# Attention on one core: a long row's scores in two joined PSUM banks, short rows and queries in a third, two banks for turned probabilities, and the inverse of long sums on GpSimd

## What is computed

```python
q = (xn @ Wq).reshape(b, n, 16, 64).transpose(0, 2, 1, 3) * 64 ** -0.5
k, v = xn @ Wkv split in two, with a null key and a null value in front
sim = einsum('bhid,bjd->bhij', q, k) + bias        # bias: 16 x 1024 x 1024
sim = where(causal, neg, sim); sim = where(mask, sim, neg)
out = einsum('bhij,bjd->bhid', softmax(sim), v)
out = layernorm(out.reshape(b, n, 1024) @ Wo)
```

## Time and profile before

| what | value |
|---|---|
| runs | 1057.35, 1048.52, 1049.11 us (median 1049.11) |
| profiled execution: span | 1055.2 us; of the runs 1057.35 us lies next above it, 2.1 us around the span |
| busy in the span | PE 88%, DVE 76%, ACT 70%, POOL 57% |
| attention with scores ahead, 64.4 to 603.5 us of the span | 539.1 us |

### The profile page before, as it was taken

One profiled execution on the slowest core, in us unless ns is written; L12 is line 12 of the kernel. 1 busy time (PEld: TensorE's weight loads), 2 busy tenths in 40 slices (PEclk: granted clock), 3 DMA queues, 4 the chain that ended last, 5 costly groups with the idle time before them and its releaser, 6 DMA issues. The chain is left out here.

```text
span 1055.2 us, 22432 instructions
## 1 busy us (share of the span) xinstructions
PE 932.6 (88%) x6180; PEld 811.6 (77%) x6180; DVE 803.2 (76%) x2324; ACT 735.9 (70%) x1651; POOL 606.0 (57%) x699
## 2 busy tenths in 40 slices
PE   7899999999999999999999966887976762599997
PEld 5578888888888898998888755677964652499996
DVE  7579989899898898998888879774757786344443
ACT  2268888888888998998999937434764652466663
POOL 2368777777776666775555525481066277344444
PEclk8879999999999999999999986888988885699999
DMA  9156656666666566675665440155864523254453
GB/s 309 44 175 180 189 171 189 178 181 180 176 184 182 170 197 182 187 199 167 182 189 171 137 150 1 51 167 148 282 178 157 205 102 138 88 78 78 73 84 48
DMA packets 111427, 162.14 MB, mean 154 GB/s; under 512 B 16201, under 2 KB 85193, under 8 KB 110282
## 3 DMA queue, kind: packets, MB, share of 16 engines
q1 hardware_dynamic: 100200, 140.56, 45.1%
q0 software_dynamic: 10224, 18.00, 8.2%
q10 hardware_dynamic: 882, 2.14, 0.6%
HBM read 110.31 MB, written 25.17 MB: 128 GB/s over the span
## 5 line engine op out<-in xcount | busy, mean ns | idle before, releaser
L2375 POOL TENSOR_SCALAR probs<-probs,inv_sum 128x1024 f32<-128x1024 f32 (+3 forms) x128 | 301.7, 2370 | 174.2 <-DVE inv_sum L2526 174.2
L2421 ACT ACTIVATE probs<-probs,neg_max 128x1025 f32<-128x1025 f32 (+7 forms) x256 | 197.5, 772 | 30.9 <-DVE neg_max L2486 29.8
L2508 DVE TENSOR_TENSOR pT_lo<-t_ps,pT_hi 128x512 fp32r<-128x512 f32 (+1 forms) x320 | 202.5, 633 | 21.3 <-ACT pT_hi L2403 20.8
L2590 PE MATMUL t_ps<-ident,probs 128*128 128x128 f32 x1152 | 179.9, 274 | 1.1 <-DVE pT_lo L2508 1.1
L2610 PE MATMUL o_ps<-pT_hi,values 128*128 128x256 f32 x576 | 175.0, 323 | 5.2 <-DVE pT_lo L2508 3.5
L2403 ACT ACTIVATE pT_hi<-t_ps 128x512 fp32r<-128x512 f32 (+1 forms) x320 | 175.5, 549 | 5.5 <-PE t_ps L2590 2.3
L2486 DVE CUSTOM_DVE_ANT_0 probs<-s_ps,bias_set,neg_null 128x512 f32<-128x512 f32 (+3 forms) x256 | 164.2, 642 | 4.5 <-PE s_ps L2559 2.6
L2590 PEld LDWEIGHTS t_ps<-ident,probs 128*128 128x128 f32 x1152 | 141.9, 141 | 31.4 <-DVE pT_lo L2508 2.7
L2611 PE MATMUL o_ps<-pT_lo,values 128*128 128x256 f32 x576 | 150.4, 281 | 0.0
L2558 PE MATMUL s_ps<-k_hi,q_hilo 128*128 128x512 f32 (+3 forms) x384 | 143.8, 375 | 4.2 <-PEq L2730 1.4
L2559 PE MATMUL s_ps<-k_lo,q_one 128*128 128x512 f32 (+3 forms) x384 | 135.4, 353 | 0.0
(11 more groups left out here) (385 smaller groups left out, 2124.7 us busy)
## 6 DMA issues: line engine op xcount, KB each, us to landing
bias_set<-bias_dram SPq DMA_DIRECT2D x16, 1024.0 KB, 5.5
bias_set<-bias_dram SPq DMA_DIRECT2D x16, 896.0 KB, 5.4
bias_set<-bias_dram SPq DMA_DIRECT2D x16, 768.0 KB, 4.9
bias_set<-bias_dram SPq DMA_DIRECT2D x16, 640.0 KB, 4.7
q_hilo<-q_hi SPq DMA_DIRECT2D x128, 64.0 KB, 2.0
q_hilo<-q_lo SPq DMA_DIRECT2D x128, 64.0 KB, 2.0
q_one<-q_hi SPq DMA_DIRECT2D x128, 64.0 KB, 2.0
bias_set<-bias_dram SPq DMA_DIRECT2D x16, 512.0 KB, 5.5
```

The lines of the kernel that those rows point to most:

```text
L2375: last = pool.tensor_scalar(keys, keys, inv_sum[:, x.set, unit, h:h + 1], None, ALU.mult)
L2421: act.activation(p, p, ACT.Exp, scale=-1.0, bias=neg_max[:, x.set, row.unit, h:h + 1], accum_out=row_sum[:, x.set, row.unit, h:h + 1]).the ...
L2508: dve.tensor_tensor(pT_lo[n % 3][:, 0:count, :], t_ps[TURNS["slot", n] % 3][:, 0:2 * P * count].rearrange("p (n q) -> p n q", n=count), pT ...
L2590: last = pe.transpose(t_ps[at % 3][:, P * (2 * m + h):P * (2 * m + h) + P], probs_row(x, row, h)[:, 1 + P * (k + m):1 + P * (k + m) + P], ...
```

## The change

- The PSUM banks are dealt out anew. `s_ps` (2 banks in a ring) and `t_ps` (3) become `long_ps` (one tile over two banks), `short_ps` (one bank) and `t_ps` (2).
- A long row of one head is scored in one piece: PE writes both chunks to `long_ps`, and one instruction of DVE (now L2502) reads up to 1024 columns, with no `part_max`. It is at slot 1 for head 0 and slot 3 for head 1.
- Short rows are at slots 2 and 4 in `short_ps`. The query uses `short_ps` too, is made for step g+3 in place of g+4, after the turn of slot 0; ACT and DVE read it in slot 1. Once a round `short_ps` takes the transposed null weights.
- `long_ps` and `short_ps` are single: a writer waits until the last use was read. With two `t_ps`, `turn(n+2)` now waits for `low(n)`.
- DVE inverts short rows only. For a long row POOL itself raises each head's sum to the power -1 and then multiplies.
- Exponentials and results on ACT come one slot later where the scores do.

```diff
-QLEAD = 4
+QLEAD = 3
...
-    for _i, _t in enumerate((0, 0, 1, 2, 3, 4)):
-        SCORES_AT[max(-1, SLOTS_A_STEP * (_x - LEAD) + _t)].append(("s", _x, _i))
+    for _t, (_unit, _h) in enumerate(((LONG, 0), (SHORT, 0), (LONG, 1), (SHORT, 1)), 1):
+        _n = max(-1, SLOTS_A_STEP * (_x - LEAD) + _t)
+        FILLS_AT[_n].append((_unit, _x, _h))
     if _x >= FIRST_Q:
-        SCORES_AT[max(-1, SLOTS_A_STEP * (_x - QLEAD) + 2)].append(("q", _x))
+        QUERY_AT[max(-1, SLOTS_A_STEP * (_x - QLEAD))].append(_x)
...
-        s_ps = [psum(st, f"s_ps{i}", [P, CW]) for i in range(2)]
-        t_ps = [psum(st, f"t_ps{i}", [P, CW]) for i in range(3)]
+        long_ps, short_ps = psum(st, "long_ps", [P, 2 * CW]), psum(st, "short_ps", [P, CW])
+        t_ps = [psum(st, f"t_ps{i}", [P, CW]) for i in range(2)]
...
# POOL, normalise(g, unit)
-                    for h in range(2) if unit == 0 else ():
-                        keys = probs_row(x, row, h)[:, 1:]
-                        last = pool.tensor_scalar(keys, keys, inv_sum[:, x.set, unit, h:h + 1], None, ALU.mult)
-                        last.then_inc(normed, 1)
+                    for h in range(2) if unit == LONG else ():
+                        pool.wait_ge(probs_ready, 4 * g + 2 * h + 1)
+                        inv = inv_sum[:, x.set, unit, h:h + 1]
+                        pool.tensor_tensor(inv, row_sum[:, x.set, unit, h:h + 1], minus_one[:], ALU.pow).then_inc(long_inv_ready, 1)
+                        pool.wait_ge(long_inv_ready, long_no(g, h) + 1)
+                        keys = probs_row(x, row, h)[:, 1:]
+                        pool.tensor_scalar(keys, keys, inv, None, ALU.mult).then_inc(normed, 1)
...
# DVE, one slot
-                    for item in SCORES_AT.get(n, ())[:1]:
-                        fill(item)
+                    for item in FILLS_AT[n]:
+                        scores(*item)
                     low(n + 1)
-                    for item in SCORES_AT.get(n, ())[1:]:
-                        fill(item)
+                    for g in QUERY_AT.get(n - 1, ()) if n else ():
+                        query(g)
...
# PE, scores(unit, g, h)
+                    if unit == LONG:
+                        ps, ready, e = long_ps, long_ready, long_no(g, h)
+                        wait(pe, long_read, e)
+                    else:
+                        ps, ready, e = short_ps, short_ready, short_no(g, h)
+                        wait(pe, short_read, e)
+                    for first, count in row.chunks:
+                        keys = slice(S * x.batch + P * first, S * x.batch + P * (first + count))
+                        to = ps[:, P * first:P * (first + count)]
+                        pe.matmul(to, q_hilo[x.set][h][:, mine], k_hi[:, keys], start=True, stop=False)
+                        last = pe.matmul(to, q_one[x.set][h][:, mine], k_lo[:, keys], start=False, stop=True)
+                    last.then_inc(ready, 1)
...
# PE, turn(n): the bank is free when slot n-2 was read, before slot n-3
-                    wait(pe, t_read, at - 2)
+                    wait(pe, t_read, n - 1)
```

More of the change, by code:

```diff
@@ L2151, in __init__ @@
         self.set = g % SETS
-        self.chunks = [(x, h, n) for x in self.rows for h in range(2) for n in range(len(x.chunks))]
         self.slots = [(x, k, n) for x in self.rows for k, n in x.slots]
-        assert len(self.chunks) == 6 and len(self.slots) == SLOTS_A_STEP
+        assert len(self.slots) == SLOTS_A_STEP and len(self.rows[1].chunks) == 1
 ALL = [Step(g) for g in range(STEPS)]
@@ L2192 @@
[L2192 to L2197, removed]
+        QUERY_AT[max(-1, SLOTS_A_STEP * (_x - QLEAD))].append(_x)
+assert QUERY_AT[-1] == [FIRST_Q]
+NULL_AT = {UNIT_SLOTS * _r + UNIT_SLOTS - 2: _r for _r in range(len(ROUNDS))}
+PROLOGUE = [("s",) + _item for _item in FILLS_AT[-1] if _item[1] == 0] + [("q", FIRST_Q)] + [("s",) + _item for _item in FILLS_AT[-1] if _item[1]]
@@ new lines, in _short_users, with long_no, short_no, exps_of @@
+def _short_users():
+    yield from (("q", i[1]) if i[0] == "q" else i[1:] for i in PROLOGUE if i[0] == "q" or i[1] == SHORT)
+    for n in range(NS):
+        if n in NULL_AT:
+            yield "null", NULL_AT[n]
+        yield from (i for i in FILLS_AT[n] if i[0] == SHORT)
+        yield from (("q", x) for x in QUERY_AT[n])
+SHORT_NO = {item: i for i, item in enumerate(_short_users())}
+def long_no(g, h):
+    return 2 * g + h
+def short_no(g, h):
+    return SHORT_NO[SHORT, g, h]
+def exps_of(n):
+    return [(ALL[g], ALL[g].rows[unit], h) for unit, g, h in FILLS_AT[n]] if 0 <= n < NS else []
@@ L2567, in query, with null_turn @@
                             t = QT * x.batch + row.tile
[L2568 removed]
+                            last = pe.matmul(short_ps[:, P * row.unit:P * row.unit + P], wq_all[:, c, 2 * x.pair:2 * x.pair + 2, :],
                                              xnT[:, c, P * t:P * t + P], start=(c == 0 and row.unit == 0), stop=(c == DC - 1),
                                              skip_group_check=True)
[L2571 to L2577 removed]
+                    last.then_inc(short_ready, 1)
+                def null_turn(r):
+                    pe.wait_ge(null_w_ready, units_done(PAIRS * (r + 1) - 1, 1))
+                    wait(pe, short_read, SHORT_NO["null", r])
+                    for unit in range(2):
+                        last = pe.transpose(short_ps[0:H, P * unit:P * unit + P], null_w[r % 2][:, unit, :], ident)
+                    last.then_inc(short_ready, 1)
                 def turn(n):
@@ L2626, in project @@
                         last.then_inc(y_ready, 1)
-                for item in SCORES_AT[-1]:
-                    fill(item)
+                for item in PROLOGUE:
+                    if item[0] == "q":
+                        query(item[1])
+                    else:
+                        scores(*item[1:])
                 for n in range(2):
```

196 lines of the change are left out of this document (88 added, 108 removed).

## The result

| what | before | after |
|---|---|---|
| median of the runs, us | 1049.9 (4 runs, 1048.5 to 1057.4) | 1193.4 (4 runs, 1189.3 to 1194.3) |
| ratio | | 1.133 [1.128, 1.138] |
| span of the profiled execution, us | 1055.2 | 1187.5 (own time 1189.3) |
| last result of the attention ready, us of the span | 616.5 | 753.9 |
| behind that, unchanged code, us | 438.7 | 433.6 |

The account below looks back on a forecast made before the run. No engine alone bound the kernel; engines waited for each other. A 7+2 step became 7.91 us PE work plus 2.70 idle, against 8.56; 62 steps gave +125.7, round ends -7: 1049.1 + 119 = 1168 us (1110 to 1220).

Parts of the forecast that it names:

- the lengthened chain: Turn and weighing wait for a remainder behind DVE's read of a whole long row: +2.05 us a 7+2 step.
- The two stalls: PE idles 1.37 us before the short row of slot 2 (query's bank), 1.24 before turn(6) in slot 4 (low(4)).
- The length of the step: Steps of 8+1, 7+2, 6+3, 5+4 blocks were to take 10.49, 10.61, 10.46, 10.18 us.
- Ends of rounds: Null turn leaves the turn banks' ring: 1 us off seven of the eight round ends, -7 us.
- The read of 896 columns: DVE's joined read of a long row: 1.14 us, or 0.13 more if crossing the bank costs a second fixed part.
- (a): Two DVE reads of scores made one: saves 0.13 us, twice a step, 0.26.
- (c): Query read a slot after it is made, so DVE's 0.59 us wait a step goes.
- POOL and SP covered: POOL's power (at most 1.56 us) and SP's query moves (landed at 8.3 us, used at 10.6) cost nothing.
- 1: Rival: PE's clock falls too, to 0.9 in the stage, 55 us more, 1222 us; chance 0.08.
- 2: Rival: only one stall stands, the query's 1.37 us, +0.86 a step, 1095 us; chance 0.11.
- 3: Rival: no change, stalls of some 0.9 us a step eat just what is saved, 1049 us; chance 0.03.
- 4: Rival: DVE is the bound, so its saving counts, 991 to 1028 us; chance 0.05.

Follow-up runs that it names:

- e1: Changed kernel, with DVE taking the query's remainder ahead of the long row's scores of slot 1: 1121.0 us, ratio 1.066 to the kernel before.
- e2: Changed kernel, with DVE in each slot taking the remainder first, then the query, then the scores: 1108.8 us, ratio 1.055 to the kernel before.
- e7: Changed kernel without the semaphore increment (mark) ahead of DVE's reads of scores: 1175.1 us, ratio 1.115 to the kernel before.
- e6: Changed kernel, with DVE reading a long row in two pieces, the first once PE has written its bank: 1210.4 us, ratio 1.146 to the kernel before.
- e8: Kernel before, with PE's query of slot 2 ahead of the turn, all banks as before: 1053.6 us, ratio 0.999.
- e4: Changed kernel, with DVE inverting long sums by a reciprocal and POOL only multiplying: 1195.8 us, ratio 1.137 to the kernel before.
- e5: As e2, and ACT's exponentials, short-row norm and results one slot later: 1098.6 us, ratio 1.040 to the kernel before.
- e3: Kernel before, with two turn banks in place of three and nothing else changed: 1101.2 us, ratio 1.049.
- e9: Kernel before without the semaphore increment (mark) ahead of DVE's reads of scores: 1049.3 us, ratio 0.998.

## Why the prediction was right, and where its sizes were off

It said slower, 1168 us (1110 to 1220), by the lengthened chain; measured 1193.4. The mechanism is the one that the runs show, and its sizes came out somewhat small. The steps one by one:

- **The two stalls.** Forecast PE idle 1.37 us for the query's bank and 1.24 for `low(4)`. The timeline shows 1.31 and 1.10 between PE's records, in the places named; counted as the forecast counts, from 0.12 us behind the start of the matmul ahead, it is 1.47 (366.60 - 365.13) and 1.26 (371.27 - 370.01). e1 removes the first alone and gets 72 us; the stall's whole recorded wait was 61 x 1.22 = 75. That stall is shown by an experiment. The second is seen in the trace, but putting the remainder ahead of the scores (e2) gave only 12 us, since ACT then became the one that DVE waits for.
- **The length of the step.** Forecast 10.49, 10.61, 10.46, 10.18; measured 10.80, 10.93, 10.83, 10.43: each 0.25 to 0.37 short. For 7+2 blocks, from the long scores' start: PE's short scores at 3.40 (forecast 3.32), the second long scores at 5.09 (4.90), turn(6) at 8.07 (7.89), turn(7) at 9.07 (8.89), the query at 9.56 (9.25), the next step at 10.93 (10.61).
- **The mis-sized terms** are three of PE's and DVE's. Short scores behind a wait take 0.34 us to the next start, not 0.24, the first matmul lasting 0.38 instead of 0.28: +0.10. From turn(7) to the query it is 0.49, not 0.36: +0.13. The earlier trace rows already had 0.44 there (305.62 - 305.18), so 0.08 of it is a reading that the forecast missed: it took the 0.36 of a turn ahead of a weighing. That turn is recorded with 0.65 us, as is the one that waited (0.66), where others last 0.60; what the remaining 0.05 is was not tested. Hand-overs from PE to DVE are 0.19 and 0.28 us, not 0.09. The forecast read 0.09 off ACT's query copy, which has no mark in front; DVE's reads have one, and by e7 it is 0.14 of the 0.19 and 0.11 of the 0.28; what else the read of slot 1 has was not tested. Against that, DVE to PE took 0.05 here, not 0.15, so the hand-overs come to +0.08 net; that the two errors cancel is luck. Together 0.31, the 0.32 that was missing, or 62 x 0.32 = 20 us. With 1 us less at the ends of rounds, +119 becomes +138, which is the stage's 137.4. The 6 us from there to 143.5 lie within the spread of the runs and are in no step.
- **Ends of rounds.** Forecast -7. The steady steps give 16 x 2.26 + 16 x 2.37 + 16 x 2.80 + 14 x 1.88 = 145 us against the 137 that the stage grew: -8.
- **The read of 896 columns** took 1.152 us, forecast 1.14. Crossing the bank costs no second fixed part.
- **(a) The joined read** was taken as a gain of 0.26 us a step, 16 us in all. e6 says 17, but the agreement is luck: there a pair of reads costs 0.44 us more than a joined one, through a gap that a remainder hid before, and gets 0.2 to 0.5 of it back by starting earlier. What joining would save in the kernel before was not run.
- **(c) The query's wait** was counted on the way to "up to 0.93 us" a step. e8, which takes away half of it in another way, gains nothing in all, so 0.59 a step was too much to count; what the change's own way of reading the query a slot later is worth was not run by itself. It did not touch the forecast, where the chain was walked. It was also read off one step; over the stage it is 26.3 us in 40 times, 0.42 a step.
- **POOL and SP covered:** right. e4 shows the power free. In the waits after, 50 to 755 us, no row has PE waiting for POOL's product (`normed`) or for the query's DMAs.
- **Rivals.** The clock did not fall (1.00 between 200 and 500 us), so 1 is out. 2 is out, both stalls stood. Its price was also wrong: it took one stall off and left the other as it was. With the query's stall gone a step of 7+2 blocks takes 9.96 us in e1 (10.93 after), as PE's waits for a turn's bank grow. Against 3 and 4 stands the result; DVE is 67% busy.

Where the 143.5 us are, in the order in which edits gave them back: 72 the query's remainder behind a long read and a remainder (e1), 12 the remainder behind the scores (e2), 10 ACT's order (e5). The last 49 are left in e5, and e3 shows that taking the third turn bank from the kernel before costs as much. The joining itself works the other way, by 17. That these last 49 are the turn bank's in the changed kernel too is not shown. The lengths of e3's and e5's steps differ, and ACT's norm ahead of a copy holds PE up in a 5+4 step of e5, so ACT's order is a rival for part of them; their cause stays open. I had given `low` ahead of the scores more than e2 found. Once that wait goes, the next engine in the ring is there within 0.2 us a step (12 us over 62 steps).

## What to carry to other kernels

Count, for each engine with a program in order, what stands ahead of the instruction that frees a buffer, and walk one step with starts and ends. A busy share of 99% and a term-by-term saving say little about a chain that goes over three engines. Price a bank before giving it away: here the third turn bank was worth 49 us in the kernel before, and the joined read 17 in the changed one. A wait removed where the next engine is nearly as late mostly changes its name: look at who is next before counting it. And look at single steps, not only at totals: e3 and e5 agree, e8 shows nothing and e6 shows 17 us, and in each of the three the steps tell something else than the sum.

## What the runs showed of the hardware

- One DVE read over two PSUM banks costs one fixed part: 885, 1019, 1152 and 1285 ns for 640, 768, 896 and 1024 columns, 133 ns per 128 and about 220 fixed, as reads in one bank have (740 for 512, 343 for 128: 132 and 210).
- A semaphore increment as an instruction of its own between DVE's wait and its read adds 0.11 to 0.14 us to a hand-over from PE (18 us in 256 reads, e7), and nothing that can be told where DVE hardly waits (e9: ratio 0.998 [0.996, 1.001]).
- A DVE read that starts from the maximum which the read ahead of it made, behind a wait and such an increment, starts 0.22 us after that maximum is out (e6), though they run on the same engine. How much of it is the increment's was not separated.
- The first PE matmul of 256 columns after a wait of 1.3 us lasts 0.38 us, in a stream 0.28, and the next starts 0.22 later instead of 0.12, at a granted clock of 1.00 in both cases (after, 366.60 and 369.78 us).
